# A binary-activation convolution: output column 0 gets an addition of its own, x is loaded in 56 columns and each pair is stored by one DMA

## The reference

```python
def _L0_conv_ref(X, W, beta, v, bias, stride):
    ...
    B = jnp.sign(W[None] - mean + us[:, None, None, None, None] * std)
    alpha = jnp.linalg.solve(Bf.T @ Bf, Bf.T @ wf)
    W_eff = jnp.einsum('m,mhwio->hwio', alpha, B)
    ...
    for n in range(N):        # N = 3
        An = jnp.sign(jnp.clip(X + v[n], 0.0, 1.0) - 0.5)
        out = out + beta[n] * (conv(An) + sum_alpha * bias[n])
    return out
...
x = x + _L0_conv_ref(_gn(x), L0_conv_W, L0_conv_beta, L0_conv_v, L0_conv_bias, 1)
```

## Time and profile before

| | us |
|---|---|
| median of 3 runs | 230.13 (229.55 to 231.52) |
| the profiled execution, its own time | 231.17 |
| its span, first to last instruction | 229.4 |

### The profile page before, as it was taken

The page is one execution under the profiler, slowest core; times in us unless marked ns, Lnnn a source line. Parts: engine busy times, 40 slices in busy tenths (PEclk is TensorE's granted clock), DMA queues, the critical chain, the costliest instruction groups (busy, mean ns, idle before and its releaser), DMA issues.

```text
span 229.4 us, 4705 instructions
## 1 busy us (share of the span) xinstructions
PE 174.2 (76%) x1812; PEld 131.7 (57%) x1812; DVE 178.5 (78%) x454; ACT 139.8 (61%) x183; POOL 10.7 (5%) x44
## 2 busy tenths in 40 slices
PE   1565015179998978969799889798888897899981
PEld 0465004076876756647577566667565665576661
DVE  5333699976889989898989898989898989784232
ACT  2349117276686868686868686868686867661130
POOL 1373000100000000000000000000000000000000
PEclk9999999999999999999999999999999999799997
DMA  5899006042355969697959797979697973749424
GB/s 121 239 262 246 3 0 141 4 97 51 73 155 149 238 193 241 206 228 195 234 172 247 212 235 196 245 204 245 188 240 186 243 200 101 190 117 252 140 76 140
DMA packets 19237, 39.60 MB, mean 173 GB/s; under 512 B 8976, under 2 KB 8976, under 8 KB 19216
## 3 DMA queue, kind: packets, MB, share of 16 engines
q1 hardware_dynamic: 18768, 39.27, 66.4%
q10 hardware_dynamic: 448, 0.04, 0.1%
HBM read 13.15 MB, written 12.85 MB: 113 GB/s over the span
## 4 chain that ended last, share of the span: by engine, by line
DVE 43%; PE 17%; issue 13%; ACT 12%; DMA 9%; SPq 5%; DVEq 0%; ACTq 0%
PE conv_ps L701 10%; DVE raw_stats L529 6%; DMA params<-in_L_conv_bias 5%; DVE s_even L585 5%; ACT signs L326 5%; DVE s_even L594 5%; PE y_ps L721 3%; ACT y_ch L339 3%; ACT x_ch L321 3%; DMA x_nat<-in_x 3%; DVE lo_part L579 3%; DVE hi_part L573 3%; DVE hi_part L578 3%; DVE lo_part L574 3%; SPq L186 3%
## 5 line engine op out<-in xcount | busy, mean ns | idle before, releaser
L326 ACT ACTIVATE signs<-x_ch,neg_thr 128x784 f16<-128x784 f32 x96 | 83.9, 939 | 33.3 <-DVE neg_thr L565 33.3
L701 PE MATMUL conv_ps<-s_even,w_mm 128*64 128x448 f16 (+1 forms) x576 | 103.8, 335 | 0.0
L704 PE MATMUL conv_ps<-s_odd,w_mm 128*64 128x448 f16 (+2 forms) x576 | 103.6, 323 | 0.0
L701 PEld LDWEIGHTS conv_ps<-s_even,w_mm 128*64 128x64 f16 x576 | 61.1, 110 | 28.7 <-issue 2.6
L704 PEld LDWEIGHTS conv_ps<-s_odd,w_mm 128*64 128x64 f16 x576 | 61.2, 111 | 0.0
L666 PE MATMUL x_ps<-ident,x_nat 112*128 112x112 f32 x224 | 33.0, 296 | 26.8 <-ACT x_ch L321 15.8
L520 DVE SCALAR_TENSOR_TENSOR y_nat<-y_ps,y_const,x_nat 112x1024 f32<-112x1024 f32 (+1 forms) x32 | 36.4, 1138 | 13.2 <-PE y_ps L721 13.2
L529 DVE BATCH_NORM_STATS2 raw_stats<-x_ch 128x6 f32<-128x448 f32 (+1 forms) x64 | 33.1, 559 | 16.1 <-ACT x_ch L321 16.1
L666 PEld LDWEIGHTS x_ps<-ident,x_nat 112*128 112x128 f32 x224 | 26.8, 161 | 31.0 <-issue 16.7
L721 PE MATMUL y_ps<-ident,y_ch 128*112 128x128 f32 x224 | 31.4, 281 | 9.9 <-DVE y_nat L520 9.9
L339 ACT ACTIVATE y_ch<-conv_ps,y_scale 128x896 f32<-128x896 f32 (+1 forms) x32 | 28.8, 900 | 16.3 <-PE conv_ps L704 9.6
(11 more groups left out here) (106 smaller groups left out, 102.9 us busy)
## 6 DMA issues: line engine op xcount, KB each, us to landing
x_nat<-in_x SPq DMA_DIRECT2D x16, 448.0 KB, 6.4
out<-y_nat SPq DMA_DIRECT2D x16, 448.0 KB, 6.6
s_odd<-s_even SPq DMA_DIRECT2D x16, 406.0 KB, 6.7
s_odd<-s_even SPq DMA_DIRECT2D x16, 377.0 KB, 6.5
x_nat<-in_x SPq DMA_DIRECT2D x16, 336.0 KB, 5.2
out<-y_nat SPq DMA_DIRECT2D x16, 322.0 KB, 2.4
s_odd<-s_even SPq DMA_DIRECT2D x16, 29.0 KB, 6.8
x_nat<-in_x SPq DMA_DIRECT2D x16, 14.0 KB, 7.3
```

The source lines that it names most:

```text
L326: act.activation(signs[q % 2][:, n, :, a, :], x_ch[q % CH_SLOTS][:, :, a, :], ACT.Sign, bias=neg_thr[q % 2][:, n, a:a + 1]).then_inc(signe ...
L701: last = nc.tensor.matmul(low[:, 0:n * ROWS], wt, s_even[b][:, part, r0:r0 + 2 * n, t:t + H], start=first, stop=end)
L704: last = nc.tensor.matmul(high[:, 0:m * ROWS], wt, s_odd[b][:, part, r0:r0 + 2 * m, t:t + H], start=first, stop=end and not at_edge)
```

## The change

x is loaded in its 56 columns only. The 57th column of `x_nat` is cleared once by GpSimd at the start. `add_x` now writes each output column to its own place in `y_nat`, and its second half writes its last 32 values (which are output column 0) into the unused 57th column. A further instruction adds column 0 out of the last 32 values of `y_ps` and column 0 of x. One DMA then stores the whole rows of a pair, behind the last of the three additions. The counts waited for follow.

```diff
-        y_nat = [sb(f"y_nat{i}", [ROWS, W * C]) for i in range(2)]
+        y_nat = [sb(f"y_nat{i}", [ROWS, (W + 1) * C]) for i in range(2)]
...
-        OUT_COLS = [slice(0, 32 * C), slice(32 * C, W * C)]
+        OUT_START = [C, 33 * C]
...
                 sp.dma_start(x_nat[s][:, IN_COLS[f]], x_pairs[q][:, IN_COLS[f]]).then_inc(loaded, 16)
-                if f == 1:
-                    sp.dma_start(x_nat[s][:, W * C:], x_pairs[q][:, 0:C]).then_inc(loaded, 16)
-
-            def store(q, f):
-                b = q % 2
-                sp.wait_ge(y_added, 2 * q + f + 1)
-                if f == 0:
-                    sp.dma_start(out_pairs[q][:, C:33 * C], y_nat[b][:, 0:32 * C]).then_inc(y_stored[b], 16)
-                else:
-                    sp.dma_start(out_pairs[q][:, 33 * C:], y_nat[b][:, 32 * C:55 * C]).then_inc(y_stored[b], 16)
-                    sp.dma_start(out_pairs[q][:, 0:C], y_nat[b][:, 55 * C:]).then_inc(y_stored[b], 16)
+
+            def store(q):
+                sp.wait_ge(y_added, 3 * q + 3)
+                sp.dma_start(out_pairs[q], y_nat[q % 2][:, 0:W * C]).then_inc(y_stored[q % 2], 16)
...
-                    store(p - 1, 0)
-                    store(p - 1, 1)
+                    store(p - 1)
...
+            for i in range(X_SLOTS):
+                pool.memset(x_nat[i][:, W * C:], 0.0).then_inc(pads_ready, 1)
...
-                at = OUT_COLS[f].start
+                at = OUT_START[f]
                 b = p % 2
+                x_at = x_nat[p % X_SLOTS]
                 dve.wait_ge(y_transposed, k + 1)
                 if f == 0 and real(p - 2):
-                    dve.wait_ge(y_stored[b], 48 * (p // 2))
+                    dve.wait_ge(y_stored[b], 16 * (p // 2))
                 stt(y_nat[b][:, at:at + 2 * n].rearrange("p (b n) -> p b n", b=2), y_ps[0:ROWS, :, 0:n],
                     y_const[0:ROWS, :],
-                    x_nat[p % X_SLOTS][:, C + at:C + at + 2 * n].rearrange("p (b n) -> p b n", b=2),
+                    x_at[:, at:at + 2 * n].rearrange("p (b n) -> p b n", b=2),
                     ALU.add, ALU.add).then_inc(y_added, 1)
+                if f == 1:
+                    stt(y_nat[b][:, 0:C], y_ps[0:ROWS, 1, n - C:n], y_const[0:ROWS, :], x_at[:, 0:C],
+                        ALU.add, ALU.add).then_inc(y_added, 1)
...
-                    pe.wait_ge(x_right[s], 32 * (q // X_SLOTS + 1))
+                    pe.wait_ge(x_right[s], 16 * (q // X_SLOTS + 1))
...
-                    pe.wait_ge(y_added, k)
+                    pe.wait_ge(y_added, 3 * p + f)
```

More of the change, by code:

```diff
@@ L224, in _ @@
             for b in range(2):
-                sp.wait_ge(y_stored[b], 48 * (PAIRS // 2))
+                sp.wait_ge(y_stored[b], 16 * (PAIRS // 2))
         @block.gpsimd
@@ L296, in _ @@
             pool.wait_ge(w_signed, M_FIL)
-            pool.wait_ge(pads_ready, 2 * S_SLOTS)
+            pool.wait_ge(pads_ready, X_SLOTS + 2 * S_SLOTS)
             pool.memset(filt[0:C, :, 1, :, 0:M_FIL], 0.0).then_inc(corners_zero, 1)
@@ L646, in _ @@
             dve.wait_ge(ratios_ready, 3)
-            dve.wait_ge(pads_ready, 2 * S_SLOTS)
+            dve.wait_ge(pads_ready, X_SLOTS + 2 * S_SLOTS)
             step(-2)
```

## The result

The changed kernel takes 236.72 us (median of 4 runs, 234.99 to 237.68) where the kernel before takes 230.09. The ratio is 1.0276, with a 95% interval of 1.0209 to 1.0342, so +6.3 us with 4.8 to 7.9. The profiled execution has 236.50 us and a span of 234.7, 5.3 us more than the span of before.

A forecast was written before the change was run, and what follows sets the result against it. The prediction took a ring of DVE and ScalarE, 11.37 us per image pair, as the bound, with x's arrival nearly as tight. Terms 1.8 + 2.9 - 1.0 + 1.4 = +5.1 on 230.13 gave 235.2 us, range 230.2 to 241.0.

The forecast's parts named there:

- a longer ring on DVE: Steady steps: DVE from L529 to neg_thr, two ScalarE signs, next L529; 11.37 us, lengthened by anything added on DVE there.
- The bound: Steady stretch, 59 to 195 us: the DVE and ScalarE ring sets the 11.37 us step; x's arrival is nearly as tight.
- The new instruction: DVE's 32-column addition in the steady steps: 0.15 us in twelve of sixteen cases, +1.8 us (0.8 to 2.6).
- x later by 1.1 us, +2.9: Steady steps: the late first-half store delays the x load 1.1 us, beyond the slack of six loads, +2.9 us.
- the lower clock: Rival, TensorE: longer gaps halve its clock, some 1.2 us lost in five of ten loads, 241 us; chance 0.13.
- The slacks: Time to spare before a late x load delays DVE's moments, for ten steady-stretch loads: 0 to 1.95 us.
- 0.2 us for the small store taken from in front of the load: SyncE, ahead of the x load: the 14 KB store's slot of 0.43 us goes, of which 0.2 was counted.
- The start: Prologue: the bias load no longer queues behind six 14 KB loads, -1.0 us (-0.3 to -2.6).
- The end: Last store: 784 KB instead of 322 KB, landing 4.1 us after issue, +1.4 us (bounds 0.9 and 2.4).
- faster than before: Rival, prologue: DVE's whole 5.14 us bias wait goes and the steady part is absorbed, 228.2 us; chance 0.06.
- the load stays inside its slack: Rival, steady steps: the later x load costs nothing; instruction, prologue and end give +2.2, 232.3 us; chance 0.28.
- a sign of being wrong: Listed signs against the forecast: steps of 11.37, x no later, clock below 1.00 between 60 and 190 us, more store pieces.

The follow-up runs named there:

- e3: Kernel before plus only the 112x32 addition behind the second-half addition, into an unused column of y_nat; 233.27 us, ratio 1.0115.
- e8: e4 with the 32-column instruction moved out of add_x, behind the three threshold instructions; 233.50 us, ratio 1.0147.
- e1: Changed kernel with its store in three again, columns 1 to 32 behind the first-half addition, the rest behind the third; 232.38 us, ratio 1.0076.
- e4: Changed kernel with the two x loads of a step issued ahead of the store instead of behind it; 233.21 us, ratio 1.0109.
- e2: Kernel before with only the first-half store also waiting for the second-half addition, three stores kept; 246.74 us, ratio 1.0583.
- e9: Changed kernel with its late store cut in two DMAs (columns 0 to 32 and 33 to 55); 240.15 us, ratio 1.0412.
- e6: Changed kernel with its store cut in three (columns 1 to 32, 33 to 55, 0), all behind the third addition; 248.51 us, ratio 1.0586.
- e7: Kernel before with the small x load replaced by a GpSimd copy of column 0 in SBUF; 229.88 us, ratio 0.9924.
- e10: e7 with the x loads issued ahead of the two second-half stores; 229.15 us, ratio 0.9956.
- e11: e6 with the small store of column 0 issued behind the two x loads instead of ahead of them; 235.57 us, ratio 1.0238.

## Why the prediction was right

The forecast was 235.2 us and 236.7 came. The mechanism is the one forecast, a longer ring on DVE and an x load that lands later behind the store; that the terms fit as well as they do is partly luck. Step by step:

- *The bound.* Right. e3 shows that 0.15 us on DVE between L529 and neg_thr lengthens every step by 0.15, and e8 that the step goes back to 11.36 when the same instruction stands outside that stretch.
- *The new instruction*, 12 x 0.15 = 1.8 us. Measured 0.15 to the next start, steps of 11.53, 1.9 us.
- *x later by 1.1 us, +2.9.* The mean wait rose by 0.8 us (9.3 to 17.3 us in ten loads), x landed 0.9 us later behind the first store ahead of it (7.9 against 7.0), and the three long steps lost 3.0 together. That this is the 2.9 forecast is luck, since two errors cancel. x was less late than taken, and it alone made some 1.8 of the 3.0; about 1.2 are the lower clock in two of the steps, which the forecast had as a rival and not in its sum. The slacks were not those of before load by load either: the forecast had six loads losing, the third most, 1.1 us; the second, fourth and tenth lost, and the third nothing (waited for 0.37 us). That the store ahead of the load is the cause is shown by e1, e4 (same bytes, other order) and e2.
- *0.2 us for the small store taken from in front of the load.* This is the term that was wrong. By its issue the load gained 0.47 us (0.38 us behind the store instead of 0.85), and in e2 and e9 the later issue reaches x; 7 us (e6) and 3 us (e9) hang on the extra stores. It did no harm to the forecast, since the changed kernel has one store; but the single store of whole rows is what kept the late first half from costing 13 us as in e2, and the forecast had not credited it.
- *The start*, -1.0 us. Measured on the bias: 24.21 to 22.95, -1.26. The working counted three of the small loads between 3.0 and 7.2 us; two are issued there, at 4.02 and 6.37 us. That it comes from the six small loads is supported by e3 and e1 (0.9 us) and e7, each near the limit of what can be measured.
- *The end*, +1.4 us. Measured 4.71 against 3.35 us from the last addition to the end of the span, +1.36: the 784 KB store, issued at 230.02, landed 4.2 us later, where 4.1 was forecast. (By its own figures the upper bound of this term is 2.3, not 2.4, and the case "faster than before" needs more than 3.2 us from the start, not 3.1; neither enters the forecast.) e4, with the whole store at the end, is slower than e1 by 0.3%: the right sign, but the intervals overlap.
- *The rivals.* That the load stays inside its slack is refuted by the three long steps and by e4. The clock does fall, in two of ten loads instead of five, and not in the longest gap. The prediction had named a granted clock below 1.00 between 60 and 190 us as a sign of being wrong, and that sign came (0.50 from 89.1 to 92.4 us): the forecast left out a real part of the loss. The start did not give 3 us.

In the profile -1.26 (start), +1.9, +3.0 and +1.36 (end) make 5.0 of the 5.3 us of span; 0.3 are not assigned. The timed runs say 6.3 with 4.8 to 7.9; the missing microsecond may lie in executions with more falls of the clock (in the four runs the two with a mean of 0.981 took 234.99 and 236.50, the two with 0.963 and 0.965 took 237.68 and 236.94), but that was not tested.

## What to carry to other kernels

Before a store is merged, ask what is queued behind it and how much slack that has, load by load and not on average: here 0.9 us of delay cost nothing in seven loads and 3.0 us of time in three, and with two more stores ahead, 1.4 us of delay, another 7 us of time. Where a load with a deadline and a store without one become ready together, issue the load first; here that was worth 1.7%, and in e10, where the first half of the store goes out early, nothing that the times show. Odd bits of work (a column that wraps round) belong on the engine that idles, not in the ring of the busiest one, even when they are only 0.15 us long: e7, with GpSimd's copy, is the version that gained, by 0.8%.

## What the runs showed of the hardware

- Each store issued ahead of the load on the same queue delayed the load's issue. x was issued 0.38, 0.85 and 1.80 us behind the first store with one, two and three stores ahead (changed kernel, e9, e2), landed 7.5, 7.4 and 7.5 us after its own issue, and the ratios were 1.028, 1.041 and 1.058 (e6, also three, 1.059). e11 does not fit this row: issued at 0.85 as in e9, x landed in 6.8 us, and the ratio was 1.024. The Trainium skill's page "DMA: Bandwidth & Descriptors", Issuing engines are not separate DMA queues, calls the time to initiate a DMA usually small relative to the DMA itself; for one DMA it is so here (0.38 us from the store's issue to the next, 5.2 us until the store has landed, page, part 6), for the kernel's time it isn't.
- With the load first and the store behind it x landed 4.2 us after its issue (e4) instead of 7.5: the store's 784 KB in front were worth 3.3 us. The Trainium skill's page "DMA: Bandwidth & Descriptors", Rules for kernel authors, asks for one large transfer and for an early issue. These runs show both at work: from three stores to one 3.1% (e6 to the changed kernel), from the store first to the load first 1.7% (changed kernel to e4).
- After gaps of 2.31 and 2.50 us in front of the transposes the clock fell to 1.2 GHz (granted 0.50 from 89.1 to 92.4 and from 184.7 to 187.5 us), after one of 2.81 us it did not (1.00 from 113.9 to 117.2 us). The length of the gap alone does not decide.
